# Where the residual's operands are made: after the key products, or beside the convolution

## The reference, cut to what is computed

```python
x_ln = layernorm(x) ; q = x_ln @ wq + bq ; q_img = q.reshape(b, c, h, w)
o = gelu(depthwise_conv7x7(q_img, dw_w, stride 2) + dw_b)         # 8x8 positions
offsets = conv1x1(o, pw_w)                                        # 2 maps of 8x8
grid = refs + tanh(offsets) ; interp = bilinear_sample(x, grid)   # 64 keys per image
k = v = interp @ wv + bv
att = softmax(heads(q @ mq_w + mq_b) @ heads(k @ mk_w + mk_b).T) @ heads(v @ mv_w + mv_b)
z = att @ mo_w + mo_b + x                                         # the residual
x1 = gelu(layernorm(z) @ mlp_w + mlp_b) + z
out = inverse_dht(threshold(block_mlp(dht2d(x1)))) + x1           # 8 blocks of 16 channels
```

## Time and profile before

| | before |
|---|---|
| median of three timed runs | 69.38 us |
| profiled execution, whole | 69.64 us |
| its span, first to last instruction on the core | 67.8 us |
| PE busy | 62.3 us (92%) |
| DVE busy | 42.2 us (62%) |
| ACT busy | 34.4 us (51%) |
| POOL busy | 30.7 us (45%) |
| DMA moved | 3.04 MB |

### The profile page before, as it was taken

How to read it: one execution, slowest core, us unless ns; L and a number is a source line. 1 busy time by engine, 2 the same in 40 slices (tenths; PEclk the granted TensorE clock), 3 DMA queues, 4 the chain that set the end, 5 groups by cost and what they waited for, 6 DMA issues and landing times.

```text
span 67.8 us, 1896 instructions
## 1 busy us (share of the span) xinstructions
PE 62.3 (92%) x776; PEld 49.9 (74%) x776; DVE 42.2 (62%) x122; ACT 34.4 (51%) x79; POOL 30.7 (45%) x39
## 2 busy tenths in 40 slices
PE   4999999999999999999799999999999859999940
PEld 4955887977879967977576859766787658999710
DVE  0092968895006859702575969568999870995650
ACT  0737675120047937749933860239740889733400
POOL 2043569999900074990799993303544400000000
PEclk9999999999999999999999999999999999999998
DMA  0779400059000000000000000000000000000054
GB/s 0 216 144 360 190 11 0 10 96 392 27 0 5 0 10 0 0 0 0 0 0 0 0 10 0 0 0 5 0 0 0 0 0 10 0 0 0 0 169 140
DMA packets 2554, 3.04 MB, mean 45 GB/s; under 512 B 361, under 2 KB 2026, under 8 KB 2546
## 3 DMA queue, kind: packets, MB, share of 16 engines
q1 hardware_dynamic: 2256, 2.78, 12.6%
q10 hardware_dynamic: 290, 0.14, 1.2%
HBM read 2.40 MB, written 0.52 MB: 43 GB/s over the span
## 4 chain that ended last, share of the span: by engine, by line
PE 81%; DVE 10%; issue 3%; POOL 1%; POOLq 1%; DVEq 0%
PE bank L813 58%; PE bank L824 13%; PE bank L991 6%; DVE rs L704 3%; PE bank L901 2%; DVE mx L696 2%; PE bank L966 2%; DVE kbr L711 1%; POOLq L171 1%; POOL rstd L434 1%; DVE u L743 1%; DVE fin L772 1%; DVE at L706 1%; DVE stats L733 1%; DVE x L750 0%
## 5 line engine op out<-in xcount | busy, mean ns | idle before, releaser
L704 DVE RECIPROCAL rs<-bank 128x256 f32<-128x256 f32 x4 | 7.0, 1758 | 3.3 <-PE bank L991 3.2
L696 DVE TENSOR_REDUCE mx<-bank 128x8 f32<-128x512 f32 x8 | 5.1, 684 | 4.1 <-PE bank L813 4.1
L813 PE MATMUL bank<-ones 128*128 128x128 f32 x22 | 6.1, 425 | 1.1 <-POOL ones L356 1.0
L813 PEld LDWEIGHTS bank<-ones 128*128 128x128 f32 x22 | 4.7, 301 | 2.2 <-issue 1.1
L515 ACT ACTIVATE pt<-bank 128x512 f32<-128x512 f32 x8 | 4.3, 591 | 3.0 <-PE bank L813 3.0
L362 POOL TENSOR_TENSOR rstd<-vareps,mhalf 128x2 f32<-128x2 f32 x4 | 3.3, 816 | 5.1 <-DVE vareps L615 5.1
L824 PE MATMUL bank<-qp,diag 128*32 128x196 f32 (+5 forms) x128 | 5.5, 330 | 0.0
L395 POOL TENSOR_TENSOR qlo<-qh,qhr 128x512 fp32r<-128x512 f32 x2 | 2.5, 1274 | 5.5 <-ACT qh L492 5.5
L824 PEld LDWEIGHTS bank<-qp,diag 128*32 128x32 f32 x128 | 4.1, 110 | 1.2
L434 POOL TENSOR_TENSOR rstd<-vareps,mhalf 128x2 f32<-128x2 f32 x4 | 2.8, 700 | 4.3 <-DVE vareps L738 4.3
L395 POOL TENSOR_TENSOR klo<-kbd,kbr 128x512 fp32r<-128x512 f32 x3 | 3.8, 1275 | 2.0 <-ACT kbr L508 2.0
(11 more groups left out here) (148 smaller groups left out, 163.5 us busy)
## 6 DMA issues: line engine op xcount, KB each, us to landing
lw<-in_late SPq DMA_DIRECT2D x1, 560.0 KB, 5.5
xt<-in_x_tok SPq DMA_DIRECT2D x4, 128.0 KB, 3.5
xc<-in_x_chan SPq DMA_DIRECT2D x1, 512.0 KB, 3.9
out_tiles<-fin SPq DMA_DIRECT2D x4, 128.0 KB, 1.8
cs<-in_const SPq DMA_DIRECT2D x1, 324.0 KB, 3.0
cs<-in_const SPq DMA_DIRECT2D x1, 280.5 KB, 5.7
ew<-in_early ACTq DMA_DIRECT2D x1, 91.5 KB, 2.7
tw<-in_taps ACTq DMA_DIRECT2D x1, 48.0 KB, 4.8
```

The costliest lines, as they stand in the source:

```text
L696: dve.tensor_reduce(mx[:, b % 2, q], ps_s[q][:].rearrange("p (i n) -> p i n", n=KEYS), AX_X, ALU.max).then_inc(s_mx, 1)
L704: dve.reciprocal(rs[:, b % 2], av_bank[b % 2][:, 256:512]).then_inc(s_rs, 1)
L813: return pe.matmul(o, lhsT, rhs, start=start, stop=stop, skip_group_check=True)
```

## The change

The addition of `ob` moves from POOL to DVE (two tensor_scalar instructions), and everything that makes the residual's operands moves in front of the end of the convolution or right behind it:

- SP waits for `s_qps` >= 2 (the query products are done) and not for `s_qimg` >= 8, and issues `xc` ahead of the second part of the constants.
- PE runs `mo` times `fb` inside the convolution, ahead of chunk 2, into column 3; `m1` times `b2k` keeps its place.
- DVE makes `ob` and adds it to the halves of `xc` between `xl` and `mlp_row`.
- ACT makes `xch` ahead of the GELU.
- POOL makes the low parts `iw` and `xcl` right after `m1`, ahead of `qlo`.

```diff
@@ sync
-            sp.wait_ge(s_qimg, 2 * PH)
+            sp.wait_ge(s_qps, 2)
+            sp.dma_start(xc[:], x_chan).then_inc(d_xc, 16)
             sp.dma_start(cs[:, SOON_N:CONST_N], const[:, SOON_N:CONST_N]).then_inc(d_const2, 16)
-            sp.dma_start(xc[:], x_chan).then_inc(d_xc, 16)
@@ gpsimd, after m1
+            tiles = [slice(4 * g, 4 * g + 4) for g in range(2)]
+            pool.wait_ge(s_iw, 2)
+            low(iw[:, 2 * C:3 * C], wmlp, iw[:, C:2 * C], s_iwl)
+            for g, t in enumerate(tiles):
+                pool.wait_ge(s_xch, g + 1)
+                low(xcl[:, t, :], xc[:, t, :], xch[:, t, :], s_xcl)
+
             pool.wait_ge(s_wt, 2)
@@ gpsimd, after keys_low(3)
-            pool.wait_ge(d_xc, 16)
-            pool.wait_ge(s_ob, 1)
-            tiles = [slice(4 * g, 4 * g + 4) for g in range(2)]
-            for t in tiles:
-                pool.tensor_tensor(xc[:, t, :], xc[:, t, :], ob[:].unsqueeze(1).broadcast_to([C, 4, P]),
-                                   ALU.add).then_inc(s_xc, 1)
-            pool.wait_ge(s_iw, 2)
-            low(iw[:, 2 * C:3 * C], wmlp, iw[:, C:2 * C], s_iwl)
-            for g, t in enumerate(tiles):
-                pool.wait_ge(s_xch, g + 1)
-                low(xcl[:, t, :], xc[:, t, :], xch[:, t, :], s_xcl)
@@ scalar
             act.copy(iw[:, C:2 * C], ps_mix[0][:, 3 * P:4 * P]).then_inc(s_iw, 1)
+            for g in range(2):
+                act.wait_ge(s_xc, g + 1)
+                act.copy(xch[:, 4 * g:4 * g + 4, :], xc[:, 4 * g:4 * g + 4, :]).then_inc(s_xch, 1)
             act.wait_ge(s_convps, 1)
...
             turned_max(2)
-            residual_high(0)
-            residual_high(1)
             exp(2)
@@ vector
+            dve.wait_ge(s_obps, 1)
+            dve.tensor_tensor(ob[:], ps_mix[1][:, 3:4], vec("mo_b"), ALU.add).then_inc(s_ob, 1)
+            dve.wait_ge(d_xc, 16)
+            dve.wait_ge(s_ob, 1)
+            for g in range(2):
+                dve.tensor_scalar(xc[:, 4 * g:4 * g + 4, :], xc[:, 4 * g:4 * g + 4, :], ob[:, 0:1], None,
+                                  ALU.add).then_inc(s_xc, 1)
+
             dve.wait_ge(s_gps, 1)
...
             dve.wait_ge(s_fb3ps, 1)
-            dve.tensor_tensor(ob[:], ps_mix[1][:, 0:1], vec("mo_b"), ALU.add).then_inc(s_ob, 1)
@@ tensor, in the convolution's loop
+                if n == 2 * CHUNK:
+                    pe.wait_ge(s_fb, 1)
+                    mm(ps_mix[1][:, 3:4], late_ap("mo"), fb[:, 2:3], start=False).then_inc(s_obps, 1)
...
             pe.wait_ge(s_fb, 1)
             pe.wait_ge(s_m1, 1)
-            mm(ps_mix[1][:, 0:1], late_ap("mo"), fb[:, 2:3])
-            mm(ps_mix[1][:, 1:2], m1[:], vec("b2k"), start=False).then_inc(s_fb3ps, 1)
+            pe.wait_ge(s_ob, 1)
+            mm(ps_mix[1][:, 1:2], m1[:], vec("b2k")).then_inc(s_fb3ps, 1)
```

More of the change, by code:

```diff
@@ L559, in products @@
                 act.copy(fl[:], ps_mix[0][:].rearrange("p (a n) -> p a n", a=4)).then_inc(s_fl, 1)
-            def residual_high(g):
-                act.wait_ge(s_xc, g + 1)
-                act.copy(xch[:, 4 * g:4 * g + 4, :], xc[:, 4 * g:4 * g + 4, :]).then_inc(s_xch, 1)
             keys(1)
```

## The result

| | before | changed |
|---|---|---|
| median | 69.42 us (4 runs, 68.61 to 70.33) | 70.86 us (4 runs, 70.10 to 70.92) |
| profiled execution, whole | 69.64 us | 70.90 us |
| its span | 67.8 us | 69.1 us |

The ratio is 1.024 (95% interval 1.016 to 1.032). A little slower had been forecast, 0.6 us and within 2%; measured were 1.44 us.

A forecast was written before the change was run, and what follows sets the result against it. The offset chain, with PE's own list level with it, was taken to bound the stretch before the sampling. Gain 0 and a cost of 0.60 us on 69.38 gave 70.0 us, range 69.1 to 71.0.

The forecast's parts named there:

- Nothing to gain at the residual: Weight load of `residual(0)` at 40.21: its 0.41 us idle is the matmul shape change and stays; gain 0, at most 0.41.
- Term 1: PE, on the path: `mo` times `fb` inside the convolution delays its end by 0.4 us, bounds 0.2 and 0.7.
- Term 2: Transfer of `xc`, hidden: issued about 12.16, landed at 16.1, a microsecond before DVE can take its first half at 17.2.
- Term 3: DVE and POOL exclude each other: additions of 0.41 us delay POOL, second `xcl` holds up `dist`; +0.60 us, otherwise +0.40.
- The slow additions: Rival: DVE's additions to `xc` take 0.93 us each, with exclusion `dist` ends +1.64 us, time 71.0; chance 0.12.
- the sum's last line: Forecast's total: median of the runs shown, 69.38, plus 0.60 gives 69.98, say 70.0 us, within 2%.

The follow-up runs named there:

- the forced overlap: Changed kernel with the `mo` times `fb` product out of the convolution and POOL's two `xcl` waiting for the first offset product; median 72.82 us, ratio 1.059.
- the product alone: Kernel before plus one 128x1 product of `mo` and `fb` in the convolution ahead of chunk 2, result unread; median 70.02 us, ratio 1.010.
- the pair with equal starts: Kernel before and changed kernel, both without the three single dummy products between query groups; medians 69.25 and 69.80 us, ratios 0.989 and 1.006.
- without the product: Changed kernel with `mo` times `fb` back in its old place, `ob` made from another, earlier column; median 70.45 us, ratio 1.022.

## Why the prediction was wrong, and where it was right

**Nothing to gain at the residual: right.** The load keeps its 0.41 us with the operands made 20 us earlier, and all profiled kernels but the one with the forced overlap take 44.6 to 44.7 us from the sampling to the end.

**Term 1: right.** 0.4 us forecast, 0.45 measured, by the change, by the product alone, and by the pair with equal starts.

**Term 2: right, but with little room.** `xc` was issued at 12.92 with 3.5 us to landing in the first trace, so it landed at 16.4. In two later ones DVE waited 0.15 and 0.20 us for it.

**Term 3: right in mechanism, its place on the path was not fixed.** DVE's first addition took 711 ns beside POOL's `iw` and the second, alone, 477 (0.41 had been estimated from `hat`); `dist` waits out an `xcl` when they meet. The additions of the first trace, and `dist` in the second and third trace of the changed kernel and with the forced overlap:

```profile
L666 DVE TENSOR_SCALAR xc<-xc,ob x2: 477/594/711, 18.1 to 18.8; 128x512 f32<-128x512 f32 x2
...
L675 DVE SCALAR_TENSOR_TENSOR dist<-th,cs x2: 425/462/498, 21.2 to 21.6; 128x256 f32<-128x256 f32 x2
...
L675 DVE SCALAR_TENSOR_TENSOR dist<-th,cs x2: 411/564/717, 20.4 to 21.1; 128x256 f32<-128x256 f32 x2
...
L675 DVE SCALAR_TENSOR_TENSOR dist<-th,cs x2: 1179/1334/1489, 20.0 to 21.1; 128x256 f32<-128x256 f32 x2
```

But I took POOL's times from one trace and PE's from the same trace as if they were tied. They aren't: the convolution's start moves with PE's rate, POOL's list with x's arrival (its `xg` begins 5.6 us behind the third pair of tiles in the traces of both kernels): the third pair of tiles reached DVE at 6.38 us in the first trace of the kernel before and at 5.81 in that of the changed kernel, whose convolution began later all the same. In the first trace of the changed kernel the two missed each other by 0.16 us, without the product by 0.3. In the second, and in the one without the dummy products, they met: `dist` asked 0.21 us before `xcl` ended and took 0.50 us, and the 0.07 us was gone again at the sampling. With the earliest start it asked 0.43 us before that end and took 0.72, and of its 0.29 us 0.20 reached the sampling. So the change costs 0.45 us, or 0.65 with an early start, where the forecast had 0.60 for all: close for the early start, and for the others by a collision that did not cost what the sum says. The slow additions, the dearest rival, did not come: 0.48 us against the 0.8 from which they would have decided.

**The step that failed is the sum's last line**, "The median of the runs shown is 0.26 us lower than that execution, 69.38, so the forecast is 69.38 + 0.60 = 69.98". It puts the difference of the two kernels' starts at nothing, without a reason. The base was the median of three runs that lay 1.7 us apart, and that spread should have been asked about before any term. In the traces with the dummy products the convolution begins anywhere from 12.7 to 14.5 us, and how long TensorE stays at its low level goes with it: the third query group is 1.08 us when it still is and 0.76 when it isn't. In the first pair of profiles the start makes 0.77 of the 1.22 us at the sampling, Term 1 the other 0.45, and of Term 3's 0.20 nothing is there. Three of the four runs of the changed kernel came at 70.8 to 70.9 us with the trace, of one of these, at 14.47; the fourth, 70.10, would by its span and the same stretches have begun near 13.7 (an estimate). That late starts came out so often was chance, as far as the runs show. Over all runs the changed kernel has a mean of 70.30 us (16 runs) and the kernel before 69.67 (94 runs, its first four left out): 0.63 us, with a standard error of 0.15; the medians, 70.17 and 69.70, differ by 0.47. These runs come from several chips; each time against the kernel before beside it, the means differ by 1.24, 0.76 and 0.44 us. The whole agrees with 0.45 to 0.65 but is too coarse to prove it; the stretches in the traces show it. The interval of the first comparison, from eight runs, excludes a cost of that size and was too narrow.

**What stays open.** What draws the start in each execution is not shown. Of the kernel before 15 of 94 runs were under 68.75 us, which would be under 69.4 with the early start's 0.65 added, and of the changed kernel 1 of 16 was (69.28); with counts so small that is no difference. The six runs without the product stay unexplained: four of them lie within what late starts give (the kernel before reaches 70.4), two at 70.8 lie above all but one of its runs, and only one execution, of 69.76 us, was profiled. A cost of the moved operands that shows in some executions only is therefore not ruled out.

**A better version.** The kernel before may not be the best one here. Without the dummy products between the query groups it had medians of 69.26 and 69.25 us beside 69.70 and 70.21 of its own, ratios 1.001 (0.987 to 1.014) and 0.989 (0.984 to 0.995). By the medians the gain is 0.4 to 1.0 us, by the means 0.56 and 0.18, and both are within 2%. The price is that 3 of 24 runs came out at 71 to 73 us. Their mean granted clock was 0.93 to 0.98, but some of the fastest runs had 0.97 too, and the changed kernel's run at 73.07 had 1.00; what made these runs slow is not shown.

## What to carry to other kernels

Work moved off engines that nobody waits for brings nothing, and what has to move with it (here one matmul of one column) may land on the path: price the small piece first, above all a full-width matmul among 32-column ones. DVE and POOL, both working from SBUF, took turns here by whole instructions, so a long POOL operation belongs where DVE has no link of a chain, and a margin of 0.2 us read off one trace is none. When three runs of a kernel lie 2% apart, find out what draws the difference before forecasting one of half that size, and compare stretches inside the traces.

## What the runs showed of the hardware

- At the start the granted clock reads 1.00 in every trace but the first one without the dummy products, while groups of 64 query matmuls take 1.08 us and later ones 0.76. The durations show the low level there, the column does not: a 128x128 product of ones takes 421 ns between 1 and 4 us, and a like product takes 420 ns at a granted clock of 0.50 (forced overlap, 26 to 30 us) and 275 at 1.00. The third group was long in the first trace of the changed kernel, the second of the kernel before and that with the product alone, and short in the others; in the two with the convolution at 12.66 and 12.67 even the first was short (0.84 us), though the program is the same up to there. PE was busy with dummy products from 0.99 us in all of them. The starts lie 2 us of 70 apart.
- PE idle for 1.78 us just ahead of 24 us was followed by some 6.5 us at the low level (0.50), which cost 2.5 us more. In the kernel before PE waits for 1.0 us at most, at the very start. At the start of two other traces (without the dummy products, the second of the kernel before and that of the change) PE idled 1.15 and 1.40 us at about 10 us, and the granted clock stayed at 1.00.
- A 128x1 float32 product costs 0.22 us among its like and 0.45 us inside a run of 32-column matmuls, so the change of shape, there and back, is about as dear as the product (0.23 us, the difference).
- The Trainium skill, SBUF — State Buffer, section Who interferes with whom, says that a DVE tensor_scalar in its two-port mode, and a DVE instruction with two SBUF inputs beside a POOL instruction that reads SBUF, contend with POOL. The traces agree in both: the tensor_scalar took 711 ns beside `iw`, 1287 ns where it waited out `abd` (change without the product) and 477 alone, though no row shows its mode; `dist` took 1.18 and 1.49 us beside `xcl` and 0.43 alone. The one that waits ends some 0.13 us earlier than the other's remaining time and its own duration alone add up to.
